# The last output projections of a windowed attention and the first feed-forward rows, in another order

## What is computed

```python
def _layer(x, wqkv, qs, ksc, wo, lg, lb, w1, b1, w2, b2):
    h = shift_token(x)
    q, k, v = split(h @ wqkv)              # 8 heads of 64
    q, k = rotary_xpos(l2norm(q) * qs, l2norm(k) * ksc)
    o = local_attention(q, k, v)           # softmax over the own and the last window
    x = x + o @ wo                         # the output projection
    h = shift_token(x)
    h = (h - mu) / sqrt(var + 1e-05) * lg + lb
    a, g = split(h @ w1 + b1)
    return x + (a * gelu(g)) @ w2 + b2
```

## Time and profile before

| | |
|---|---|
| median of 3 runs | 3050.54 us (3049.99 to 3052.98) |
| the profiled execution, its own time | 3057.01 us |
| its span, first to last instruction | 3055.2 us |
| TensorE matmuls busy | 2993.7 us, 98% |
| TensorE weight loads busy | 2437.0 us, 80% |
| VectorE, ScalarE, GpSimd busy | 53%, 40%, 37% |
| granted TensorE clock, mean | 0.993 |

### The profile page before, as it was taken

How to read it: one execution, slowest core, us unless ns; L and a number is a source line. 1 busy time by engine, 2 the same in 40 slices (tenths; PEclk the granted TensorE clock), 3 DMA queues, 4 the chain that set the end, 5 groups by cost and what they waited for, 6 DMA issues and landing times. The chain is left out here.

```text
span 3055.2 us, 44311 instructions
## 1 busy us (share of the span) xinstructions
PE 2993.7 (98%) x17096; PEld 2437.0 (80%) x17096; DVE 1612.3 (53%) x3359; ACT 1230.9 (40%) x2497; POOL 1131.8 (37%) x1200
## 2 busy tenths in 40 slices
PE   7999999999999999999999999999999999999999
PEld 6787888888878887888877888888878778787777
DVE  5975667766764333333324667766665333333332
ACT  5864555555554111111123555555565211111111
POOL 6755556655641110111103655666551111121111
PEclk8999999999999999999999999999999999999999
DMA  6642111111131111010122111111123111111110
GB/s 232 202 161 78 42 43 46 56 42 53 35 117 46 42 42 42 32 33 20 42 91 61 32 43 53 48 47 39 53 77 110 52 42 35 39 55 52 43 53 26
DMA packets 142582, 187.75 MB, mean 61 GB/s; under 512 B 21094, under 2 KB 74858, under 8 KB 142372
## 3 DMA queue, kind: packets, MB, share of 16 engines
q1 hardware_dynamic: 142372, 184.92, 18.9%
HBM read 132.44 MB, written 52.46 MB: 61 GB/s over the span
## 5 line engine op out<-in xcount | busy, mean ns | idle before, releaser
L938 PE MATMUL quad<-fhT_f,w_h_f 128*128 128x512 f32 (+1 forms) x1392 | 551.1, 396 | 1.5 <-ACT w_h_f L988 1.5
L940 PE MATMUL quad<-fhT_f,w_l_f 128*128 128x512 f32 (+1 forms) x1392 | 545.2, 392 | 0.0
L939 PE MATMUL quad<-fhT_f,w_h_f 128*128 128x512 f32 (+1 forms) x1392 | 543.8, 391 | 0.0
L1559 DVE SCALAR_TENSOR_TENSOR u_f<-quad,bias_f,gate_f 128x512 f32<-128x512 f32 (+1 forms) x174 | 130.2, 749 | 632.1 <-PE quad L940 557.0
L1139 ACT ACTIVATE lprob<-lprob,small 128x384 f32<-128x384 f32 (+2 forms) x512 | 288.6, 565 | 155.7 <-DVE small L1425 155.6
L1713 POOL TENSOR_TENSOR turned_qk<-with_cos,with_sin 128x256 f32<-128x256 f32 x256 | 188.7, 758 | 425.7 <-DVE with_cos L1450 369.2
L720 PE MATMUL bank_pair<-wqkv_h,hT 128*128 128x512 f32 x1024 | 330.8, 404 | 0.5 <-DVE with_sin L1450 0.5
L988 ACT ACTIVATE uT_f<-u_f 128x512 fp32r<-128x512 f32 (+1 forms) x176 | 111.3, 632 | 540.7 <-DVE u_f L1559 532.6
L1235 ACT ACTIVATE gate_f<-quad,bias_f 128x512 f32<-128x512 f32 (+1 forms) x174 | 119.5, 687 | 507.9 <-PE quad L940 507.9
L940 PEld LDWEIGHTS quad<-fhT_f,w_l_f 128*128 128x128 f32 (+1 forms) x1392 | 256.8, 184 | 63.0
L938 PEld LDWEIGHTS quad<-fhT_f,w_h_f 128*128 128x128 f32 (+1 forms) x1392 | 257.1, 185 | 60.8 <-ACT w_h_f L988 2.4
(11 more groups left out here) (201 smaller groups left out, 6108.5 us busy)
## 6 DMA issues: line engine op xcount, KB each, us to landing
s_in<-stream SPq DMA_DIRECT2D x128, 128.0 KB, 2.8
s_res<-stream SPq DMA_DIRECT2D x64, 256.0 KB, 2.8
stream<-a_out SPq DMA_DIRECT2D x64, 256.0 KB, 2.0
res_f<-stream SPq DMA_DIRECT2D x63, 256.0 KB, 3.0
w_h_f_raw<-in_L_ffn_w SPq DMA_DIRECT2D x60, 256.0 KB, 5.3
h_in_f<-stream SPq DMA_DIRECT2D x112, 128.0 KB, 2.3
x_in<-in_x SPq DMA_DIRECT2D x32, 256.0 KB, 2.8
ctx_in<-in_ctx SPq DMA_DIRECT2D x32, 256.0 KB, 3.0
```

What stands on the lines that cost most here:

```text
L938: e.matmul(bank[0:n, :], high, hT[:, 0, c, :], start=c == 0, stop=False)
L939: e.matmul(bank[0:n, :], high, hT[:, 1, c, :], start=False, stop=False)
L940: ins = e.matmul(bank[0:n, :], low, hT[:, 0, c, :], start=False, stop=c == KC - 1)
L1559: e.scalar_tensor_tensor(out=Fm.u[q % 2][0:n, :], in0=up_bank(2 * (g * HC + j) + 1)[0:n, :], scalar=Fm.bias1[0:n, 0, j:j + 1], in1=Fm.gate ...
```

## The change

Four things change their place, in both layers:

- The output projection of tile 28, in step 31 around the turning of q and k, goes to the first half of step 32: one half of it behind the scores of tile 30, the other behind the turned probabilities of tile 29.
- Its residual add on VectorE goes from the end of step 31 to the end of the first half of step 32, behind the rope products of tile 31.
- The turning of early rows 0 and 1 goes from the first half of step 32 to the second, behind the scores of heads 4 to 7 of tile 30. Their splits on ScalarE and VectorE go along; they stand ahead of VectorE's divisions and behind its maxima.
- Rows 0 to 3 now use the two halves of `bank_pair` in turn, and the waits of `turn_early` follow from that.

SyncE's program is not touched.

```diff
     def early_bank(t):
-        return (banks[0], bank_pair[:, 0, :], bank_pair[:, 0, :], bank_pair[:, 1, :])[t]
+        return bank_pair[:, t % 2, :]
...
                     w.wait_ge(S("a_out"), n)
-                    if t == TILES - 3:
-                        w.wait_ge(S("fhT_low"), base + 1)
...
+                    if (s, d) == (TILES, 0):
+                        project_out(tail - 1, 0)
                     if (s, d) == (TILES, 1):
+                        turn_early(l, 0)
+                        turn_early(l, 1)
                         project_out(tail, 0)
...
                     if (s, d) == (TILES, 0):
-                        turn_early(l, 0)
-                        turn_early(l, 1)
+                        project_out(tail - 1, 1)
...
-                    if d and ended and s != TILES:
+                    if d and ended and s not in (TILES - 1, TILES):
                         project_out(tail, 0)
...
-                    if d and ended and s != TILES + 1:
+                    if d and ended and s not in (TILES - 1, TILES + 1):
                         project_out(tail, 1)
...
             w.wait_ge(S("early_again"), 16 * GROUP * (l + 1))
-            if t == 0:
-                w.wait_ge(S("v_rows"), (l + 1) * TILES)
-                w.wait_ge(S("a_out"), (l + 1) * TILES - 3)
-            elif t == 2:
-                w.wait_ge(S("fhT_low"), n)
+            if t < 2:
+                w.wait_ge(S("with_sin"), 2 * (l + 1) * TILES - 1 + t)
             else:
-                w.wait_ge(S("with_sin"), 2 * (l + 1) * TILES - (t == 1))
+                w.wait_ge(S("fhT_low"), n - 1)
...
+                    if (s, d) == (TILES, 1):
+                        split_normalised(l, 0, early_bank(0))
+                        split_normalised(l, 1, early_bank(1))
                     if live:
                         divide(t, 2 * d)
...
-                    if d and ended:
+                    if d and ended and s != TILES - 1:
                         add_residual(tail)
-                    if s == TILES:
-                        split_normalised(l, 2 * d, early_bank(2 * d))
-                        split_normalised(l, 2 * d + 1, early_bank(2 * d + 1))
+                    if (s, d) == (TILES, 0):
+                        add_residual(tail - 1)
+                    if (s, d) == (TILES, 1):
+                        split_normalised(l, 2, early_bank(2))
+                        split_normalised(l, 3, early_bank(3))
```

## The result

| | before | after |
|---|---|---|
| median, 7 runs each | 3050.73 us (3048.70 to 3053.61) | 3060.94 us (3059.76 to 3061.74) |
| ratio, 95% interval | | 1.0029 [1.0019, 1.0039] |
| the profiled execution, its span | 3057.01 us, 3055.2 us | 3060.35 us, 3058.6 us |
| TensorE waiting for early rows | 4.7 us in two waits | 15.0 us in two waits |

What follows compares the result with a forecast made beforehand. TensorE, busy 98% of the span, was taken as the bound. First layer 3.5 - 0.2 + 2.5 = 5.8 us, second 3.3 - 0.2 + 2.5 = 5.6, together +11.4 on 3050.5: 3062 us, range 3054 to 3066.

Steps and rivals of the forecast that it cites:

- k of tile 30 turned 1.8 us earlier: Step 31, first layer: with the projection gone, k is turned at 852.3 and not 854.12, TensorE 1.8 us earlier.
- 7.30 us from the add to the rows: First layer: delay from the end of tile 28's residual add to the first early-row transpose, 7.30 us, kept after the change.
- sum of 7.4 us: Alternative total for both layers if early loads land 2.6 us after issue, as the Trainium skill estimates: 11.4 - 4.0 = 7.4 us.
- 7.92 us in the second layer: Second layer: delay from the end of tile 28's residual add to the first early-row transpose, 7.92 us, kept after the change.
- The projection of tile 29 3.5 us later: Step 32, first layer: behind the eight late transposes it starts at 872.8 and not 869.28, 3.5 us later.
- The clock, 2.5 us a layer: Behind the long early-row wait: work slowed by the low clock costs 2.5 us a layer, taken between 1.7 and 3.4.
- 1.7 us for before: Step 32 of the kernel before: 3.4 us at half speed behind the two waits, costed as 1.7 us lost.
- Sum at the place: Steps 31 and 32, both layers: added time of 5.8 us in the first and 5.6 in the second, +11.4 us.
- TensorE is the bound as everywhere, so nothing gives it back: Behind steps 31 and 32: TensorE still bounds the kernel, so the added +11.4 us stays in the total.
- (a): Rival, faster: early rows are there when TensorE reaches them at 864.0; -9.4 us, 3041 us; chance 0.09.
- (b): Rival, little changed: wait without a clock fall, 6.4 us, 3057 us, or shorter landings, down to 3053; chance 0.14.
- (c): Rival, slower still: low clock beyond 6.7 us or a second wait in step 33; 3070 us; chance 0.07.

Runs made afterwards that it cites:

- e4: Changed kernel with VectorE's residual add of tile 28 put later still, behind the maxima of heads 4 to 7 of tile 30; 3069.14 us, ratio 1.0062.
- e6: Kernel before with only the output projection and residual add of tile 28 moved, early rows left where they were; 3069.14 us, ratio 1.0055.
- e0_after_again: The changed kernel itself, unedited, run once more beside the kernel before; 3061.38 us, ratio 1.0034.
- e1_loads_first: Changed kernel with SyncE's store of tile 28 and residual load of tile 30 put behind the four early loads; 3046.72 us, ratio 0.9985.

## Why the prediction was right, point by point

Forecast 3062, range 3054 to 3066, measured 3060.94. The direction and the mechanism were right. That the size is so near is in part luck: the places gave +7.5 where the sum had 11.4, two of its terms were too large, and a third part, which it didn't have, made up for most of that.

- *k of tile 30 turned 1.8 us earlier.* From the start of the place it was turned at 854.12 - 849.59 = 4.53 us before and at 848.07 - 845.37 = 2.70 after: 1.83. The other 1.2 us of the 3.0 taken out were idled away, as said; the brackets name half of that (0.34 for ScalarE's copies, 0.27 for GpSimd).
- *TensorE at the early rows at 864.0,* 14.4 us behind the start of the place. Measured 860.0 - 845.37 = 14.6.
- *The add ends at 864.5,* 14.9 us behind. Measured 860.25 - 845.37 = 14.88.
- *7.30 us from the add to the rows.* Measured 867.52 - 860.25 = 7.27. This chain carried the prediction. That it held to a tenth is luck: in the second profile of the same kernel it took 6.80 us, and 6.88 to 7.05 in e4 and e6. VectorE's and TensorE's rows of e0_after_again:

```profile
858.00 0.68 DVE L1465 TENSOR_TENSOR a_out<-bank,s_res 128x512 f32<-128x512 f32 x1
```

```profile
865.48 1.97 PE L627 MATMUL bank_pair<-ident,h_in_f 128*128 128x128 f32 x8 [7.04 <-DMA h_norm_f<-early]
...
869.75 1.47 PE L819 MATMUL quad<-ident,lprob 128*128 128x128 f32 x12
```

  The estimate by the Trainium skill (DMA: Bandwidth & Descriptors, section Anatomy of one DMA, for one transfer on the GpSimd path), 2.6 us from the last issue, is not borne out for the last of four loads on this queue: from the end of the last issue, 862.99, to the use of the rows are 4.5 us, and the list of transfers gives 4.1 for such a load with nothing right behind it. Its sum of 7.4 us is close to the +7.5 of the places by accident.
- *7.92 us in the second layer.* Measured 2276.96 - (2269.06 + 0.68) = 7.22, from VectorE's row

```profile
2269.06 0.68 DVE L1465 TENSOR_TENSOR a_out<-bank,s_res 128x512 f32<-128x512 f32 x1
```

  The term was 0.7 us too large. The row of before that made the difference I hadn't looked at: one pair of issues took 1.78 us there, where it takes 0.86 elsewhere. SyncE's queue before, second layer:

```profile
2263.86 1.78 SPq L367 DMA_DIRECT2D h_in_f<-early  x2
```

- *Waits of 7.8 us, 15 to 17 us in total.* Measured 7.52, 7.46 and 15.0.
- *The projection of tile 29 3.5 us later.* It starts 23.77 us behind the start of the place (869.14 - 845.37) and not 19.69: 4.1, of which 0.6 belong to the clock term, since the eight transposes took 1.62 us (867.52 to 869.14) and not 1.03. That leaves 3.5.
- *The clock, 2.5 us a layer:* **the term that was mis-sized.** The stretches of the changed kernel around the end of the wait:

```profile
863.00:864.00 1.00, 0.00 (x0) 0.00 (x0) 0.00 (x0) 0.85 (x4) 1.00 (x2) 0.81 1.13 350
...
867.00:868.00 1.00, 0.48 (x2) 0.48 (x3) 0.00 (x0) 0.00 (x0) 0.00 (x0) 0.50 1.09 340
...
869.00:870.00 1.00, 1.00 (x5) 0.90 (x4) 0.69 (x1) 0.75 (x2) 0.00 (x0) 0.50 1.16 321
870.00:871.00 1.00, 1.00 (x5) 0.77 (x5) 0.81 (x3) 0.13 (x1) 0.00 (x0) 0.78 1.06 285
```

  The clock is at 0.50 from 863.6 (the mean of that microsecond is 0.81) to 870.4, 6.8 us, as long as the upper bound that I took from the earlier trace rows. But 3.9 of these lie inside the wait, where TensorE has nothing to slow down. It worked for 2.9 us at 1.2 GHz: 0.6 us lost in the transposes and 0.6 in the half projection (869.14 to 871.23, 2.09 us, against 1.48 to 1.5), **1.2 us** and not 2.5. The step took the length of the low clock for the length of slow work. In two layers that is 2.6 us too much. How much of it falls on work changes with the execution: in e0_after_again it is also some 6.8 us long, but from the rows (865.48) to the next probabilities (869.75) are 4.27 us and not 3.71, so 1.75 us were lost there. The same slip, but small, is in the prediction's 1.7 us for before: from mixing to the projection are 869.28 - 865.01 = 4.27 us, against 1.46 + 1.26 at the full clock, so 1.55 were lost.
- *Sum at the place:* 11.4 less 2.6 (clock) and 0.7 (second layer's delay) is 8.1; measured 7.5. Of the last 0.6, 0.2 are two short waits that are gone and were costed short or not at all (0.28 for maxima and 0.16 for `oT` in the second layer, against the 0.2 taken); the other 0.4 isn't located.
- *"TensorE is the bound as everywhere, so nothing gives it back":* nothing did. But something was added, 2 to 2.7 us beyond the place, which no step had. It made up for most of what the other terms had too much: the total is nearer to the forecast than its parts, by luck. With the places alone the time would have been 3058, the lower end of the forecast's own range.
- *The weight loads, nothing:* TensorE waited for no weights at the place.

The rivals. (a), that the rows would be there, is refuted for this queue, and e1_loads_first is what it described: it gave 3041 for loads that go out ahead of the add, measured were 3046.7 for that very edit. It left out that ScalarE's copies would be late next, and what the moved projection costs outside the place. (b) was right that the fall of the clock may in part miss the work, and at the places the result (+7.5) is nearer to its 6.4 without the clock term than to the forecast's 11.4. The time of (c), 3070, came only in e4_add_later and e6_projection_only (3069), and there by a longer first wait: no second wait above 0.4 us came behind it, and the low clock lasted longer (some 10 us), mostly within the wait.

## What to carry to other kernels

When an operation moves, look up who waits for its result on an in-order queue, and what stands behind the waiting entry there: here an add with no hurry of its own held four loads that TensorE needed first, at about one microsecond of the place for each microsecond of the add, and another order in the queue's program turned a loss of 9.5 us into a gain of 5.2. Cost a stretch of low clock by the work that falls into it and not by its length. And compare kernels of this length between two markers of the same work in their traces, since the spans of two profiled executions hid 7 of the 10 us here.

## What the runs showed of the hardware

- The same wait does not always bring the clock down. 2.06 and 2.10 us of waiting at the same matmul of the same kernel left it at 1.00 in one execution and brought it to 0.50 in another; the feed-forward part was 1.55 us longer there, and 1.2 in the mean of all profiles. A long wait (7.0 to 7.5 us, both layers of both profiles of the changed kernel) brought it down within the wait, and cost 1.2 to 1.75 us of slower work afterwards; with 9.8 us of waiting in e4_add_later the clock came back 3.6 us after work did (869.88 to 873.5, by its stretches of 2 us).
- Four 256 KB loads issued in a row land 2.8 us (the first pair) and 4.1 us (the second) after their issue with nothing right behind them (e1_loads_first; 3.7 to 4.2 for the second pair in four such kernels), where a single load of that size takes 2.9 and a single store 2.0.
- Profiled executions of programs that are the same up to step 31 reached it at times 5.8 us apart (843.8 to 849.6), as much as the effect of half of these experiments.
